# A recommendation tower on one core: the high parts of ten tables written to PSUM as well, and subtracted from there

## What is computed

```python
e = jnp.stack([tbl_0[ids[:, 0]], ..., tbl_26[ids[:, 26]]], axis=1)   # 2048 x 27 x 128
dot = jnp.einsum('bnd,bmd->bnm', e, e)      # of which the pairs i < j are kept: z
h = jnp.concatenate([z, dense_ctx], axis=1)
h = jnp.maximum(h @ W_top1 + b_top1, 0.0)
h = jnp.maximum(h @ W_top2 + b_top2, 0.0)
y = h @ W_top3
```

## Time and profile before

| | us |
|---|---|
| median of 3 runs | 641.28 |
| lowest and highest | 640.8, 643.16 |
| the profiled execution | 642.85 |
| its span, first to last instruction | 641.0 |

### The profile page before, as it was taken

The page is one execution under the profiler, slowest core; times in us unless marked ns, Lnnn a source line. Parts: engine busy times, 40 slices in busy tenths (PEclk is TensorE's granted clock), DMA queues, the critical chain, the costliest instruction groups (busy, mean ns, idle before and its releaser), DMA issues.

```text
span 641.0 us, 9183 instructions
## 1 busy us (share of the span) xinstructions
PE 404.4 (63%) x3768; PEld 341.8 (53%) x3768; DVE 215.7 (34%) x462; ACT 97.9 (15%) x190; POOL 260.6 (41%) x272
## 2 busy tenths in 40 slices
PE   5888315263739992819271999371808089955997
PEld 3667204152628891718161888261707078845996
DVE  6898003010109960301010797010101059801220
ACT  2442001010111210102020212010201012110322
POOL 6778763544540027363645001737273600072000
PEclk9899557585959996758685999666767579985999
DMA  8983313131414202223222230123232325010322
GB/s 224 248 213 93 82 49 69 49 81 38 97 37 91 61 13 53 55 67 62 61 62 60 49 103 8 50 44 86 39 84 45 77 34 114 9 50 23 59 48 36
DMA packets 71137, 45.23 MB, mean 71 GB/s; under 512 B 53100, under 2 KB 59628, under 8 KB 71096
## 3 DMA queue, kind: packets, MB, share of 16 engines
q1 hardware_dynamic: 60578, 25.80, 18.0%
q0 software_dynamic: 8448, 17.32, 10.7%
q10 hardware_dynamic: 2070, 1.53, 1.0%
HBM read 38.75 MB, written 5.87 MB: 70 GB/s over the span
## 4 chain that ended last, share of the span: by engine, by line
PE 54%; issue 33%; DVE 4%; another core or an unknown queue 3%; DMA 3%; SPq 1%; ACT 1%; ACTq 0%
PE ps_hot L710 12%; PE ps_hot L664 10%; PE ps_hot L666 9%; PE ps_h L723 6%; PE ps_dot L710 6%; PE ps_tr L692 5%; PE ps_h L745 3%; DVE onehot L478 3%; DMA dots<-in_tbl 2%; PE ps_h L766 2%; PE ps_hot L681 1%; PE ps_hot L682 1%; DVE table_lo L444 1%; DMA dots_scratch<-dots 1%
## 5 line engine op out<-in xcount | busy, mean ns | idle before, releaser
L434 POOL DMA_INDIRECT rows<-in_tbl,cold_ids x264 | 259.7, 984 | 320.6 <-PE ps_tr L692 237.9
L710 PE MATMUL ps_hot<-eT 128*54 128x54 f32 x1024 | 77.2, 261 | 214.7 <-issue 195.3
L710 PEld LDWEIGHTS ps_hot<-eT 128*54 128x54 f32 x1024 | 59.1, 171 | 232.5 <-issue 211.9
L478 DVE TENSOR_SCALAR onehot<-hot_ids,row_number 125x512 fp32r<-125x512 int32 x336 | 146.8, 485 | 4.7 <-PE ps_hot L666 2.6
L664 PE MATMUL ps_hot<-onehot,table_hi 125*128 125x512 f32 x336 | 134.2, 399 | 14.8 <-DVE onehot L478 10.9
L666 PE MATMUL ps_hot<-onehot,table_lo 125*128 125x512 f32 x336 | 132.9, 396 | 0.0
L231 DVE COPY dots<-ps_hot 128x432 f32<-128x432 f32 x16 | 9.7, 608 | 238.3 <-remote 131.7
L664 PEld LDWEIGHTS ps_hot<-onehot,table_hi 125*128 125x128 f32 x336 | 64.2, 191 | 33.1 <-issue 17.6
L666 PEld LDWEIGHTS ps_hot<-onehot,table_lo 125*128 125x128 f32 x336 | 64.2, 191 | 13.1
L494 DVE COPY eT<-ps_tr 128x512 f32<-128x512 f32 (+1 forms) x36 | 23.3, 648 | 111.6 <-remote 56.4
L723 PE MATMUL ps_h<-zT,w 128*128 128x128 f32 x360 | 50.6, 281 | 0.0
(11 more groups left out here) (39 smaller groups left out, 140.0 us busy)
## 6 DMA issues: line engine op xcount, KB each, us to landing
hot_ids<-in_hot_ids SPq DMA_DIRECT2D x40, 256.0 KB
dots_scratch<-dots SPq DMA_DIRECT2D x62, 87.8 KB
rows<-in_tbl,cold_ids POOLq DMA_INDIRECT x264
zT<-dots_scratch SPq DMA_DIRECT2D x47, 58.5 KB
w<-in_tbl SPq DMA_DIRECT2D x3, 448.0 KB
dots<-in_tbl SPq DMA_DIRECT2D x2, 560.0 KB
dots<-in_tbl SPq DMA_DIRECT2D x2, 448.0 KB
w<-in_tbl SPq DMA_DIRECT2D x1, 560.0 KB
```

The source lines that it names most:

```text
L434: pool.indirect_dma_start(out=rows[k % NR][:, f, :], out_offset=None, in_=x["cold"][f][:, :], in_offset=bass.IndirectOffsetOnAxis(ap=cold_ ...
L478: dve.tensor_scalar(onehot[:, c % NO, :], hot_ids[h % NI][0:CR, :], row, None, ALU.is_equal).then_inc(onehot_ready, 1)
L710: last = pe.matmul(banks[k][SC * c:SC * c + WN, WN * g:WN * g + WN], e.rearrange("d a b -> d (a b)"), e.rearrange("d a b -> d b a"), start ...
```

## The change

For every table but the first, `split_high` rounds the staged table a second time, into PSUM, and signals `hi_ready` only after that; `split_low` subtracts the PSUM copy in place of `table_hi`. A table of 1280 numbers per partition needs two and a half banks, so `ps_tr` and `ps_h1` become one tensor of three banks, `ps_dot` and `ps_h2` another, and the tables take turns between the two. From the third on, ACT must wait until DVE has subtracted the table that lay there before (`lo_ready` of h-2). The memsets of `ps_dot` and PE's wait for them go. The copies of products out of PSUM take 118 partitions, those that the products fill, where they took 128.

```diff
+        ps_tr_h1 = ps("ps_tr_h1", [P, 3, 4, P])
+        ps_dot_h2 = ps("ps_dot_h2", [P, 3, 4, P])
+        apart = [bank.rearrange("p a c d -> p (a c) d")[0:CR] for bank in (ps_tr_h1, ps_dot_h2)]
...
-            of = banks[k][:, 0:BS * WN].rearrange("p (g w) -> p w g", w=WN)
-            return copy(dots[i][:, :, BS * k:BS * k + BS], of)
+            of = banks[k][0:SC + WN, 0:BS * WN].rearrange("p (g w) -> p w g", w=WN)
+            return copy(dots[i][0:SC + WN, :, BS * k:BS * k + BS], of)
...
-                dve.tensor_tensor(in_table(table_lo, h, part), staging[h][:, a:b], in_table(table_hi, h, part),
+                high = apart[h % 2][:, 0:CHUNKS[h]] if h else in_table(table_hi, h, part)
+                dve.tensor_tensor(in_table(table_lo, h, part), staging[h][:, a:b], high,
                                   ALU.subtract).then_inc(lo_ready, 1)
...
-            for i in range(2):
-                dve.memset(ps_dot[i][:, :], 0.0).then_inc(cleared, 1)
...
-                act.copy(in_table(table_hi, h, part), staging[h][:, a:b]).then_inc(hi_ready, 1)
+                high = act.copy(in_table(table_hi, h, part), staging[h][:, a:b])
+                if h:
+                    if h > 2:
+                        act.wait_ge(lo_ready, splits(h - 2))
+                    high = act.copy(apart[h % 2][:, 0:CHUNKS[h]].bitcast(f32r), staging[h])
+                high.then_inc(hi_ready, 1)
...
-                if first and t == 0 and q == 1:
-                    pe.wait_ge(cleared, 4)
```

More of the change, by code:

```diff
@@ L154, in dlrm_tower @@
         ps_hot = [ps(f"ps_hot{i}", [P, ST * P]) for i in range(2)]
-        ps_tr = [ps(f"ps_tr{i}", [P, TG, P]) for i in range(2)]
-        ps_dot = [ps(f"ps_dot{i}", [P, ST * P]) for i in range(2)]
-        ps_h1 = ps("ps_h1", [P, M1, P])
-        ps_h2 = ps("ps_h2", [P, 4, P])
+        ps_tr_h1 = ps("ps_tr_h1", [P, 3, 4, P])
+        ps_dot_h2 = ps("ps_dot_h2", [P, 3, 4, P])
+        apart = [bank.rearrange("p a c d -> p (a c) d")[0:CR] for bank in (ps_tr_h1, ps_dot_h2)]
+        ps_tr = [ps_tr_h1[:, i] for i in range(2)]
+        ps_dot = [ps_dot_h2[:, i].rearrange("p c d -> p (c d)") for i in range(2)]
+        ps_h1 = ps_tr_h1[:, 2]
+        ps_h2 = ps_dot_h2[:, 2]
         last_h1 = [ps_hot[0][:, 0:P], ps_hot[1][:, 0:P], ps_tr[0][:, 0, :], ps_tr[1][:, 0, :]]
```

## The result

The changed kernel is slower on the chip on which both were first timed: 669.63 us, median of six runs (667.69 to 671.68), against 642.05 us for the kernel before (six runs, 640.8 to 643.94). The ratio is 1.042, with a 95% interval of 1.039 to 1.045; the cost is 27.6 us. Forecast was a gain of 4. The profiled execution took 671.68 us, its span is 669.9 us, and the mean granted TensorE clock is 0.771.

The account below looks back on a forecast made before the run. POOL's pace over its first 48 gathers was taken to set the whole chain. Gains of 3.6 us in long gathers and 0.4 us in PE's lag, all else 0, took 641.3 to 637.3 us; range 635.3 to 642.0.

Parts of the forecast that it names:

- the cover: Room of the hot lookups ahead of the 49th gather, 11.7 us, then 7.7; hides ACT's added roundings at cost 0.
- the sum itself: Whole kernel: -3.6 - 0.4 = -4.0 us, from a median of 641.3 to 637.3 us.
- The 3.6 us: POOL's first 48 gathers: gain once subtractions from PSUM no longer hold up four long gathers; computed 3.3 to 4.7 us.
- more gathers gain: Rival: gathers beside the other six subtractions gain too and the lag shrinks by 1.2 us; -5.9, 635.4 us; chance 0.11.
- 0.4 us for PE's lag behind the last gather: Tile 3's last gather to PE free: the 4.9 us shrink, gain 0.4 us, bounds 0 and 1.2.
- steps: Rival: PE's creeping takes its 44 steps whatever POOL does, so PE's arrival counts; 3.5 us lost, 644.8; chance 0.07.
- frees nothing: Rival: a subtraction's PSUM input frees nothing for POOL, whose pace stays; 641.3 us (640.3 to 642.5); chance 0.24.
- No gather over 1.5 us among the first 40: Sign of being right, on POOL: the long gathers of 1.62 to 2.41 us are gone.
- The 49th gather near 70.8 with 0.30 us idle: Sign of being right: tile 3's first gather, at 74.36 before, starts near 70.8 without POOL waiting for PE's transposes.
- The last of tile 3 near 90.4: Sign of being right: POOL's last gather for tile 3, which ended at 94.02 before, ends near 90.4.
- The q = 1 products of tile 0 near 95: Sign of being right: PE starts this half of tile 0 near 95; PE was free at 98.90 before.
- Transposes between 61.6 and 65: Sign of being right: PE's transposes of tile 0, at 61.60 before, start at most slightly later.

Follow-up runs that it names:

- e9: The changed kernel as it is, on a chip without late signals: 377.52 us, ratio 0.9872 to the kernel before.
- e10: The kernel before as it is, traced on a chip without late signals: 382.72 us, ratio 1.0023.
- e13: The changed kernel with the subtraction reading `table_hi` in SBUF again, on a chip without late signals: 382.67 us, ratio 1.004.
- e1: The changed kernel with only the subtraction's operand put back to `table_hi` in SBUF, on a chip with late signals: 644.16 us, ratio 1.0003.
- e4: The kernel before, with POOL waiting after each four gathers of a tile until they have landed, with late signals: 527.53 us, ratio 0.8155.
- e2: The changed kernel with a POOL memset behind each gather of tiles 0 to 2, on a chip with late signals: 643.82 us, ratio 1.0007.
- e6: The kernel before with at most two gathers under way, on a chip without late signals: 516.7 us, ratio 1.347.
- e11: The changed kernel with at most four gathers under way, on a chip without late signals: 399.68 us, ratio 1.0468.
- e12: The changed kernel with at most eight gathers under way, on a chip without late signals: 378.34 us, ratio 0.9926.
- e15: The kernel before with at most eight gathers under way, on a chip without late signals: 382.81 us, ratio 1.0031.

## Why the prediction was wrong

**What was right.** That a subtraction with two SBUF inputs holds up a gather and one with a PSUM input doesn't: the longest of the first 40 gathers takes 1.22 us in the changed kernel, where four took 1.62 to 2.41. e9, e10 and e13 show it both ways. The Trainium skill says of this, in "SBUF — State Buffer", section "Who interferes with whom", two things that differ: an instruction with two SBUF inputs holds what GpSimd needs too, and a `tensor_tensor` was seen not to hold up DMA issued by GpSimd. The measurement decides for the first: 2.41, 2.42, 2.33 us beside such subtractions in e10, none over 1.35 in e9. That ACT's roundings (1.01 us for 1024 numbers into PSUM, against the SBUF price of 1.05 that I took), the memsets, 118 partitions (607 ns, where 128 took 608) and the joined banks cost next to nothing: e1 and e13, ratios 1.0003 and 1.004 (1.0002 to 1.0077). That the roundings put tile 0's transposes back by 1 to 3 us and the cover takes it, on a chip without late signals: 63.44 in e9 against 62.16 in e10, with the 49th gather at 69.22. That a DVE subtraction reading PSUM takes no longer than one reading SBUF: 1.21 us for 1024 numbers in both. And the sum itself, on chips where POOL's pace does set the end: 4.9 us gained (2.8 to 6.9), forecast 4.0, in part by luck, as the next paragraph shows.

**The 3.6 us were too few as a gain of POOL's.** Without late signals POOL won 6.9 us by the 49th gather. I had counted four long gathers from one execution; e10 has six. That was the rival "more gathers gain", whose 5.9 us is within the interval of e9 as the forecast is. The price of 1.28 us for an ordinary gather was too high as well: the other 32 of that stretch average (43.48 - 8.44) / 32 = 1.10, by which the four alone give 4.1 us. The other term, 0.4 us for PE's lag behind the last gather, has no place on such a chip, where nothing creeps.

**The step that failed is the cover.** I wrote that the lookups have 11.7 us of room ahead of the 49th gather, 7.7 once POOL is faster, and that 3.5 us would show "if the cover were gone", "no more". PE came not 1 to 3 us later to tile 0's transposes but 41.6. The bound was built from one thing alone, ACT's extra work, because I took the lookups' pace for given. Under it lay a reading of the earlier trace rows: that PE creeps in the small products while gathers are issued. Right was "while gathers are issued" (in e4 it gets going in most of POOL's pauses, one to three us after the last gather). Wrong was the place. In the lookups PE's signals come late, and DVE and ACT wait for them; in the products PE itself goes forward in steps of 0.70 us. That both are one backlog I take from the common step and from their beginning and ending with the gathers; no run shows it. The kernel before issued a gather per 1.55 us in the lookups and stayed free of it, with e1 (POOL held up by subtractions again) and e2 (POOL held up by a memset) as its two neighbours at 644 us; the changed kernel issues one per 1.25 to 1.5 there and falls in. The margin is small: over the first 24 gathers the mean is 1.46 us before and 1.34 after. So the 0.3 us of stall per gather, which I had counted as lost time to be won back, was what kept the lookups free. The profile of the kernel before had the question open to view: 195.3 us "issue", and my text said that the profile doesn't say why. I went on to use it as if its extent were known.

**The rival "steps"** had PE's arrival count in place of POOL's pace, and that it did: the 49th gather was released by PE's transposes, the sign that I had named for the cover gone. But its creeping was still the products', so its price of 3.5 us was short by 24, and 0.07 was all that I gave to "slower". **The rival "frees nothing"** falls with e9.

**The signs.** No gather over 1.5 us among the first 40: right. The 49th gather near 70.8 with 0.30 us idle: 104.07 with 38.24; on a chip without late signals it is 69.22 with 0.30. The last of tile 3 near 90.4: 123.77. The q = 1 products of tile 0 near 95: 116.90. Transposes between 61.6 and 65: 103.19; without late signals 63.44. The 3.7 to 4.9 us behind a tile's last gather: tile 3's last ends at 123.77, PE is free at 126.78, so 3.0.

**What stays open.** Why some chips have late signals and others don't; what in a gather by index delays them; why in steps of 0.70 us; and at what pace of gathers, or beside what, the lookups fall in. On a chip with late signals the changed kernel was run only for the first result, and with e4's pauses not at all, so whether the change costs anything beside the pauses is open too. All executions here were recorded ones. In those with late signals the page gives no time from issue to landing for any gather, and 3.1 us in e9 and e10. It gives none either in e6, e11, e12 and e15, without late signals, where gathers share their semaphores otherwise, so this alone says little; whether recording has part in the late signals, no run here can tell.

No version is best everywhere. With late signals the kernel before with pauses after each four gathers took 527.5 us (ratio 0.8155); without them the changed kernel as it is took 377.5 (ratio 0.9872), and the pauses would cost it 145.

## What to carry to other kernels

A large idle time that the profile leaves unexplained is no constant: before you speed up the engine that it goes along with, ask what happens if it spreads to the stretches that were free of it, and leave room for that in the range. A stall on an engine that isn't needed soon can be a brake that others live by; giving the engine a useless memset for that time is a quick test of it. Subtract from PSUM where GpSimd issues gathers beside VectorE and its pace sets the end, and time both kernels on more than one chip.

## What the runs showed of the hardware that was not expected

- The kernel before takes 642 to 644 us on some chips (3, 10 and that of the first result) and 381.5 to 382.8 on others (0, 11, 15), with a mean granted clock of 0.787 in the one profile and 0.991 in the other.
- On the first kind, beside gathers by index, a finished matmul's signal can reach VectorE and ScalarE 19 us late (49.84 to 69.09); the delay grows while gathers are issued (6.75 us at 35.39), and what it releases goes in steps of about 0.70 us. Plain loads of as many packets and bytes from the same queue bring none of it: 380.4 against 643.9 us on the same chip.
- Pauses of GpSimd help (527.5 us), and so, less, does spacing the gathers (629.3); a limit of four under way that hardly ever binds doesn't (653.8).
